# Four unread products ahead of each quad's gate and up, from quad 15 on

## Chip, cores and metric

The kernel runs on one core of one Trainium2 chip. The metric is the device time of one execution in microseconds, the median of several runs.

## What is computed

One layer on x of 16 x 256 tokens with 128 features: cross attention (16 heads of 8) to a context of 64 positions, added to x, and then a mixture of experts behind a second layer norm: a shared expert, and 64 routed experts of which each token takes 6. The routed half is what the change touches:

```python
x = x + xattn(layernorm(x), ctx_768, Wq, bq, Wk, bk, Wv, bv, Wo, bo)
x = x + moe(layernorm(x))
# moe, T = 4096 tokens, E = 64 experts, K = 6 a token, in 8 groups of which 4 stay
shared = silu(x @ sg_w.T) * (x @ su_w.T) @ sd_w.T
scores = sigmoid(x @ gate_w.T) + gate_bias
topk_w, topk_i = top_k(scores * group_mask, 6); topk_w /= topk_w.sum() + 1e-8
h = silu(einsum('th,eih->eti', x, eg_w)) * einsum('th,eih->eti', x, eu_w)
routed = einsum('eti,ehi,te->th', h, ed_w, comb)
out = shared + routed
```

## The kernel before

The program has one hand-ordered stream of instructions for each engine, tied by semaphores. It has three parts.

*Attention and routing, 16 batches.* For each batch of 256 tokens the attention is computed, the six experts of each token are picked, and GpSimd (POOL) scatters each token's row to its place in the array `pages` in HBM (L403). A page has 128 rows, in two halves of 64 rows, and each half belongs to one expert. In all there are 224 pages, taken four at a time: 56 quads (`NQ`).

*The shared expert* for all batches, in banks `bank_r` and `bank_w` of PSUM. The last two batches are finished inside quad 0; their sums (`sh_added`) are the last use of these two banks.

*The quads.* All weights of the experts lie in SBUF. For quad q:
- SP loads the pages (L344) once the buffer of quad q - 4 is free (`packed` from DVE, `pxt_done` from PE), and stores the results of quad q - 6 behind it (L332).
- PE transposes the four pages (`page_x`, L1091) into PSUM, ACT copies them to `pxt` (L455).
- DVE packs the experts' numbers (L986, L989). DVE and ACT copy the weights of these experts to `gu_now` and `d_now`, half each (DVE L1003, L1010; ACT L455).
- PE multiplies: gate and up (`gate_up`, 8 products, shown as 16 instructions writing `bank_s`), ACT takes the silu (`s_act`, L616), DVE multiplies with the up half (`h_t`, L1038), PE computes the down product (`down`, shown as 8 instructions to `bank_o` or `bank_q`), ACT copies the result to `y_s`.

PE's order in the loop is gate_up(q), page_x(q+1), down(q-1). ACT's order is silu(q), page copy(q+1), result copy(q-1), weights of quad q+2. DVE's is pack(q+2), h_t(q), weights of quad q+2, and then, in every second quad from `FIRST_SUM` = 15 on, `combine(n)` (L1022): the six results of each token of tile n, weighted, are added to `xb`.

POOL's part after the scatters is `gather(n)` for 32 tiles of 128 tokens: six indirect DMAs (L436) that fetch the six result rows of each token from `results` in HBM. A tile's gathers wait until the quads they need are stored, and, as there are four buffers, until the sum of tile n - 4 is made. 21 sums lie in the loop of the quads (quads 15, 17, ... 55), 11 behind it.

`mm(dst, w, v)` (L1095) is the helper by which most products are recorded, so the groups on its line are told apart by the tiles they write.

Of the kernel before, what the change touches and what calls it, by code (L numbers as in the profile page):

```python
# [19 lines left out]
BF16 = mybir.dt.bfloat16  # L20
# [6 lines left out]
P = 128  # L27
B = 16
# [30 lines left out]
FIRST_SUM = (E // HALVES + FILL) // QUAD + 4  # L59
# [18 lines left out]
def build(nc, x, ctx_cols, wq, bq, wk, bk, wv, bv, wo, bo, gate_cols, gate_bias, expert_gu, expert_d, shared_gu, shared_d, out, pages, results):  # L78
    with ExitStack() as ctx:
        def sb(name, shape, dt=F32):  # L80
            return ctx.enter_context(nc.sbuf_tensor(name, shape, dt))

        def ps(name, cols):
            return ctx.enter_context(nc.psum_tensor(name, [P, cols], F32))

        def sem(name):
            return ctx.enter_context(nc.semaphore(name))
# [6 lines left out]
        bank_w = ps("bank_w", 512)  # L94
# [14 lines left out]
        before = sb("before", [P, P])  # L109
        before_h = sb("before_h", [P, P], BF16)  # L110
        ones_h = sb("ones_h", [P, P], BF16)
        head_mask = sb("head_mask", [P, NH])
        mask_r = sb("mask_r", [P, HR])
        below = sb("below", [P, HR])
# [124 lines left out]
        sh_in, sh_silu, sh_ready, sh_done, sh_added = sem("sh_in"), sem("sh_silu"), sem("sh_ready"), sem("sh_done"), sem("sh_added")  # L239
# [410 lines left out]
        def _(dve):  # L650
            dve.memset(empty[:, :, :], 0.0).then_inc(empty_ready, 1)
            dve.wait_ge(made, MADE)
            dve.memset(fill[:, :], 0.0)
            dve.memset(ones_h[:, :], 1.0)
            for g in range(QUAD):
                dve.memset(digit[:, g:g + 1], float(E ** g))
            for j in range(2):
# [429 lines left out]
        def _(pe):  # L1087
            def transposes(outs, ins, done):
                for o, i in zip(outs, ins):
                    k = i.shape[0]  # L1090
                    last = pe.transpose(o, i, ident[0:k, 0:k])  # L1091
                last.then_inc(done, 1)

            def mm(dst, w, v):
                return pe.matmul(dst, w, v, start=True, stop=True)  # L1095

            def transpose_x(n):
                pe.wait_ge(xn_ready, TPB * (n + 1))
                if n > 0:
                    pe.wait_ge(q_ready, n)  # L1100
                    pe.wait_ge(kexp_ready, HR * n)
                    pe.wait_ge(vblk_ready, 2 * n)
                transposes([bank_q[:, t * P:(t + 1) * P] for t in range(TPB)], [xn[:, t, :] for t in range(TPB)], xt_done)
# [97 lines left out]
            def filling_body(b):  # L1201

                values(b - 1)
                if on(b - 3):
                    count_choosers(b - 3)
                transpose_x(b + 2)
                if on(b - 2):
                    transpose_x2(b - 2)
                    logits(b - 2)
                transpose_back(b - 1)  # L1210
                transpose_max(b)
                transpose_o(b - 1)
                shifted_scores(b)
                out_projection(b - 1)
                project(b + 2)
                scores(b + 1)

            def body(b):
                if filling(b):
                    filling_body(b)  # L1220
                    return
                if on(b - 1):
                    values(b - 1)
                if on(b + 2):
                    transpose_x(b + 2)
                if on(b - 3):
                    count_choosers(b - 3)
                if on(b - 1):
                    transpose_back(b - 1)
                if on(b):  # L1230
                    transpose_max(b)
                if on(b - 2):
                    transpose_x2(b - 2)
                if on(b):
                    shifted_scores(b)
                if on(b - 2):
                    logits(b - 2)
                if on(b + 2):
                    project(b + 2)
                if on(b + 1):  # L1240
                    scores(b + 1)
                if on(b - 1):
                    transpose_o(b - 1)
                    out_projection(b - 1)
# [12 lines left out]
            def page_x(q):  # L1257
                j = q % SLOTS
                pe.wait_ge(page_in[j], 16 * (q // SLOTS + 1))
                transposes([xt_ps[q % 2][:, g * P:(g + 1) * P] for g in range(QUAD)], [pg[j][:, g, 0:D] for g in range(QUAD)],  # L1260
                           pxt_done)

            def gate_up(q):
                pe.wait_ge(pxt_ready, q + 1)
                pe.wait_ge(gu_lower, q + 1)
                pe.wait_ge(gu_upper, q + 1)
                for u in range(HALVES * QUAD):
                    g, h = divmod(u, HALVES)
                    last = mm(gu_ps[q % 2][:, u * U:(u + 1) * U], gu_now[q % 2][:, g, h, :], pxt[q % 2][:, u * U:(u + 1) * U])
                last.then_inc(gu_done, 1)  # L1270

            def down(q):
                pe.wait_ge(h_ready, HALVES * (q + 1))
                pe.wait_ge(d_lower, q + 1)
                pe.wait_ge(d_upper, q + 1)
                if q >= 2:
                    pe.wait_ge(y_ready, q - 1)
                for g in range(QUAD):
                    last = mm(y_ps[q % 2][:, g * D:(g + 1) * D], h_t[q % 2][:, g, :, :].rearrange("p h t -> p (h t)"), d_now[q % 3][:, g, :])
                last.then_inc(y_done, 1)  # L1280
# [8 lines left out]
            def shared_down(b):  # L1289
                pe.wait_ge(sh_ready, b + 1)  # L1290
                if 2 <= b < SHARED_LATE:
                    pe.wait_ge(sh_added, b - 1)
                out_bank = (sh_out if b < SHARED_LATE else sh_bank)[b % 2]
                for t in range(TPB):
                    end = mm(out_bank[:, t * D:(t + 1) * D], sh_h[b % 2][:, t * P:(t + 1) * P], sd_t[:, :])
                end.then_inc(sh_done, 1)
# [17 lines left out]
            pe.wait_ge(sh_added, SHARED_LATE)  # L1314
            pe.wait_ge(h_zeroed, 2)
            for q in range(NQ):
                gate_up(q)
                if q + 1 < NQ:
                    page_x(q + 1)
                if q > 0:  # L1320
                    down(q - 1)
                if q == 0:
                    for b in range(SHARED_LATE, B):
                        shared_down(b)
# [32 lines left out]
```

## Time and profile before

| | |
|---|---|
| median of 3 runs | 854.12 us (847.09, 854.12, 857.15) |
| the profiled execution | 851.24 us, span 849.3 us |
| mean granted TensorE clock | 0.685 |
| PE busy | 488.6 us (58%), 2996 products and 2996 weight loads |
| DVE busy | 452.5 us (53%) |
| POOL busy | 388.8 us (46%) |
| ACT busy | 356.1 us (42%) |
| HBM traffic | 98 GB/s over the span |

The span is the time from the first to the last instruction on the core; the device time has 1.9 us around it. PE is the matrix engine (TensorE), DVE is VectorE, ACT ScalarE, POOL GpSimd, SP the engine that only issues DMAs here. The granted clock is a share of full speed: 1.00 is 2.4 GHz and 0.50 is 1.2 GHz. A product's end is modelled in the profile, its start is recorded. In the views by time, a row merges neighbouring instructions of one kind, and square brackets give the idle time of that engine ahead of it and what is taken to have ended it ("remote" and "issue": nothing that the profile shows).

### The profile page before, as it was taken

The page shows a single profiled execution, that of the slowest core. Times are in us where ns is not written, and L with a number is a line of the kernel's source. Part 1 is how long each engine was busy: PE and PEld are TensorE (multiplying, and loading weights), DVE is VectorE, ACT ScalarE, POOL GpSimd, SP SyncE. Part 2 cuts the span into 40 slices and gives each one's busy share as a digit, 9 for nine tenths or more (in the row PEclk, how much of TensorE's full clock was granted, in tenths as well). Part 3 has the DMA queues.
Part 4 walks back from the last instruction along what each step waited for, and adds up shares of the span by engine and source line. Part 5 has one row for each costly group of instructions (what it writes and reads, how often), then busy time and mean ns, then how long its engine had stood idle before and what let it go on. Part 6 is the DMA issues. An engine that isn't in the chain of part 4 may idle for free.

```text
span 849.3 us, 11843 instructions
## 1 busy us (share of the span) xinstructions
PE 488.6 (58%) x2996; PEld 408.4 (48%) x2996; DVE 452.5 (53%) x2313; ACT 356.1 (42%) x1002; POOL 388.8 (46%) x425
## 2 busy tenths in 40 slices
PE   4776555544476655322789866547777686674000
PEld 2554333323244433212679855547777686674000
DVE  4586665555666666564366633336555455455322
ACT  4563443433334433221169843436555555553000
POOL 2016455445655455566400253453444453445774
PEclk9975655567855555555799955768676867877555
DMA  7433221222222222121225532334444444433321
GB/s 217 159 128 106 91 95 51 77 97 100 101 100 94 91 94 63 60 66 47 82 63 138 150 100 76 99 99 127 114 121 110 116 130 107 118 104 84 83 59 49
DMA packets 89747, 84.25 MB, mean 99 GB/s; under 512 B 10256, under 2 KB 76816, under 8 KB 89680
## 3 DMA queue, kind: packets, MB, share of 16 engines
q1 hardware_dynamic: 76272, 57.93, 22.9%
q0 software_dynamic: 12288, 25.29, 10.5%
q8 instruction: 24, 0.39, 0.2%
q14 instruction: 43, 0.35, 0.1%
q10 hardware_dynamic: 1120, 0.28, 0.1%
HBM read 39.21 MB, written 44.25 MB: 98 GB/s over the span
## 4 chain that ended last, share of the span: by engine, by line
issue 30%; POOL 26%; PE 21%; ACT 9%; another core or an unknown queue 7%; DVE 4%; ACTq 1%; POOLq 0%; DMA 0%; DVEq 0%
POOL pages L403 17%; PE bank_s L1095 10%; PE bank_q L1095 4%; POOL empty L436 4%; POOL p_t L436 3%; ACT d_now L455 3%; PE bank_s L1091 2%; PE bank_o L1095 2%; POOL rstd L393 2%; ACT pxt L455 2%; ACT gu_now L455 2%; ACT s_act L616 1%; PE bank_r L1095 1%; ACTq L455 1%
## 5 line engine op out<-in xcount | busy, mean ns | idle before, releaser
L1095 PE MATMUL bank_s<-pxt,gu_now 128*128 128x64 f32 x896 | 148.3, 336 | 96.0 <-ACT pxt L455 61.0
L1095 PEld LDWEIGHTS bank_s<-pxt,gu_now 128*128 128x128 f32 x896 | 143.2, 250 | 103.0 <-ACT pxt L455 66.7
L436 POOL DMA_INDIRECT p_t<-results,place_i x96 | 90.9, 947 | 155.0 <-DMA results<-y_s 78.4
L436 POOL DMA_INDIRECT empty<-results,place_i x96 | 90.7, 945 | 89.4 <-DVE xb L1022 46.5
L1038 DVE TENSOR_TENSOR h_t<-bank_s,s_act 64x256 f32<-64x256 f32 x112 | 47.8, 427 | 134.5 <-ACT s_act L616 70.1
L403 POOL DMA_INDIRECT pages<-payload,place_i x96 | 93.3, 972 | 37.7 <-issue 27.6
L403 POOL DMA_INDIRECT pages<-pg,place_i x96 | 92.8, 966 | 31.3 <-issue 27.6
L393 POOL TENSOR_TENSOR rstd<-ve,minus_half 128x4 f32<-128x4 f32 (+1 forms) x21 | 18.5, 880 | 137.9 <-DVE ve L870 136.3
L616 ACT ACTIVATE s_act<-bank_s 64x512 f32<-64x512 f32 x56 | 33.0, 590 | 84.2 <-remote 63.6
L1194 PE MATMUL bank_o<-bias_s,ident 128*128 128x256 f32 x32 | 18.0, 661 | 82.4 <-ACT o_t L455 74.3
L477 ACT ACTIVATE p_t<-bank_s 128x512 f32<-128x512 f32 x64 | 35.6, 599 | 51.2 <-issue 26.4
L455 ACT ACTIVATE gu_now<-w_gu 128x128 f32 x224 | 51.0, 297 | 3.4 <-DVE expert_i L989 1.8
L1010 DVE COPY d_now<-w_d 64x128 f32 x224 | 36.1, 221 | 29.9 <-remote 17.6
L455 ACT ACTIVATE d_now<-w_d 64x128 f32 x224 | 50.4, 294 | 1.4
L1194 PEld LDWEIGHTS bank_o<-bias_s,ident 128*128 128x128 f32 x32 | 7.4, 288 | 88.3 <-ACT o_t L455 78.6
L1091 PE MATMUL bank_s<-ident,pg 128*128 128x128 f32 x224 | 46.2, 345 | 0.0
L1022 DVE SCALAR_TENSOR_TENSOR xb<-empty,weight,xb 128x128 f32<-128x128 f32 x96 | 33.6, 350 | 23.6 <-DMA empty<-results,place_i 20.8
L1022 DVE SCALAR_TENSOR_TENSOR xb<-p_t,weight,xb 128x128 f32<-128x128 f32 x96 | 33.7, 352 | 21.4 <-DMA p_t<-results,place_i 18.5
L1095 PE MATMUL bank_q<-d_now,h_t 128*128 128x128 f32 x224 | 44.3, 365 | 0.7 <-issue 0.7
L455 ACT ACTIVATE pxt<-bank_s 128x512 f32<-128x512 f32 x56 | 33.0, 590 | 26.3 <-remote 15.1
L822 DVE SCALAR_TENSOR_TENSOR picked<-iota_e,expert_f,row 128x64 f32<-128x64 f32 x192 | 42.1, 274 | 2.8 <-issue 2.8
L1095 PEld LDWEIGHTS bank_q<-d_now,h_t 128*128 128x128 f32 x224 | 42.5, 282 | 0.8 <-issue 0.8
(161 smaller groups left out, 1033.6 us busy)
## 6 DMA issues: line engine op xcount, KB each, us to landing
pg<-pages SPq DMA_DIRECT2D x56, 258.0 KB
results<-y_s SPq DMA_DIRECT2D x56, 256.0 KB
pages<-empty SPq DMA_DIRECT2D x18, 774.0 KB
w_gu<-in_expert_gu SPq DMA_DIRECT2D x16, 256.0 KB
w_d<-in_expert_d SPq DMA_DIRECT2D x32, 128.0 KB
out_x<-xb SPq DMA_DIRECT2D x16, 128.0 KB
xb<-in_x SPq DMA_DIRECT2D x3, 512.0 KB, 8.1
pages<-payload,place_i POOLq DMA_INDIRECT x96
```

Source lines behind the costliest of these rows:

```text
L393: pool.tensor_tensor(rstd[b % 2][:, part], ve[:, part], minus_half[:, part], ALU.pow).then_inc(rstd_done, 1)
L403: pool.indirect_dma_start(out=pages[:, :], out_offset=bass.IndirectOffsetOnAxis(ap=place_i[:, TPB * n + t, k:k + 1], axis=0), in_=payload[ ...
L436: pool.indirect_dma_start(out=ys[n % YS_SLOTS][:, k, :], out_offset=None, in_=results[0:landed * QUAD * P, :], in_offset=bass.IndirectOffs ...
L455: return act.activation(dst, src, ACT.Copy)
L477: act.activation(p_t[:, c, :], chunk[c], ACT.Exp).then_inc(p_ready, 1)
L616: act.activation(s_act[:, :, :, :].rearrange("p g h t -> p (g h t)"), gu_ps[q % 2][0:INTER, :], ACT.Silu).then_inc(act_ready, 1)
L822: place_step(n, ("pick", t, k), dve.scalar_tensor_tensor(out=picked[:, k, :], in0=iota_e[:, :], scalar=expert_f[:, t, k:k + 1], in1=row[:, ...
L1010: copied = dve.tensor_copy(d_now[q % 3][0:INTER, g, :], w_d[0:INTER, bass.ds(e, 1), :].rearrange("p e h -> p (e h)"))
L1022: part = dve.scalar_tensor_tensor(out=xt, in0=ys[n % YS_SLOTS][:, k, :], scalar=weight[:, n, k:k + 1], in1=xt, op0=ALU.mult, op1=ALU.add)
L1038: dve.tensor_tensor(h_t[q % 2][h * INTER:(h + 1) * INTER, :, h, :], gu_ps[q % 2][INTER:2 * INTER, :].rearrange("p (g h t) -> p g h t", g=Q ...
L1091: last = pe.transpose(o, i, ident[0:k, 0:k])
L1095: return pe.matmul(dst, w, v, start=True, stop=True)
```

## The change

DVE fills a new tile of ones, `warm_in` (128 x 512, bfloat16), at the start. From quad 15 on PE computes, ahead of each quad's gate_up and so behind the down product of the quad before the last, four products of the ones `ones_h` (128 x 128) with `warm_in` into `bank_w`. They wait for nothing, and nothing reads them. At quad 15 PE waits once until all 16 shared sums are made, the last reads of that bank. `NQ` is 56, so 41 quads have them: 164 products.

```diff
--- before.py
+++ after.py
@@ -109,6 +109,7 @@
         before = sb("before", [P, P])
         before_h = sb("before_h", [P, P], BF16)
         ones_h = sb("ones_h", [P, P], BF16)
+        warm_in = sb("warm_in", [P, 4 * P], BF16)
         head_mask = sb("head_mask", [P, NH])
         mask_r = sb("mask_r", [P, HR])
         below = sb("below", [P, HR])
@@ -652,6 +653,7 @@
             dve.wait_ge(made, MADE)
             dve.memset(fill[:, :], 0.0)
             dve.memset(ones_h[:, :], 1.0)
+            dve.memset(warm_in[:, :], 1.0)
             for g in range(QUAD):
                 dve.memset(digit[:, g:g + 1], float(E ** g))
             for j in range(2):
@@ -1094,6 +1096,11 @@
             def mm(dst, w, v):
                 return pe.matmul(dst, w, v, start=True, stop=True)
 
+            def keep_busy(times):
+
+                for _ in range(times):
+                    mm(bank_w[:, :], ones_h[:, :], warm_in[:, :])
+
             def transpose_x(n):
                 pe.wait_ge(xn_ready, TPB * (n + 1))
                 if n > 0:
@@ -1314,6 +1321,10 @@
             pe.wait_ge(sh_added, SHARED_LATE)
             pe.wait_ge(h_zeroed, 2)
             for q in range(NQ):
+                if q == FIRST_SUM:
+                    pe.wait_ge(sh_added, B)
+                if q >= FIRST_SUM:
+                    keep_busy(4)
                 gate_up(q)
                 if q + 1 < NQ:
                     page_x(q + 1)
```

## Rows read from the trace of the kernel before
**Rows 1.** stretch, us, busy PE, PEld, DVE, ACT, POOL, granted clock, DMA, GB/s

```profile
425.00:500.00 75.00, 59.81 (x462) 56.27 (x460) 41.51 (x205) 54.77 (x179) 11.37 (x12) 0.92 0.42 110
500.00:780.00 280.00, 197.56 (x1152) 193.10 (x1152) 136.91 (x606) 142.56 (x443) 124.51 (x132) 0.72 0.41 109
780.00:849.30 69.30, 0.00 (x0) 0.00 (x0) 23.76 (x68) 0.60 (x1) 45.71 (x49) 0.51 0.27 69
```

**Rows 2.** PE in order of time: start, us, what, count [idle before]

```profile
585.84 2.67 PE L1095 MATMUL bank_s<-pxt,gu_now 128*128 128x64 f32 x16 [2.13 <-issue]
...
605.48 3.51 PE L1095 MATMUL bank_s<-pxt,gu_now 128*128 128x64 f32 x16
...
655.68 1.91 PE L1095 MATMUL bank_q<-d_now,h_t 128*128 128x128 f32 x8
657.39 2.50 PE L1095 MATMUL bank_s<-pxt,gu_now 128*128 128x64 f32 x16
...
660.17 1.06 PE L1095 MATMUL bank_o<-d_now,h_t 128*128 128x128 f32 x8
665.00 3.27 PE L1095 MATMUL bank_s<-pxt,gu_now 128*128 128x64 f32 x16 [3.78 <-ACT pxt L455]
...
668.92 1.91 PE L1095 MATMUL bank_q<-d_now,h_t 128*128 128x128 f32 x8
...
691.05 2.13 PE L1095 MATMUL bank_s<-pxt,gu_now 128*128 128x64 f32 x16 [1.48 <-ACT pxt L455]
...
693.83 1.91 PE L1095 MATMUL bank_q<-d_now,h_t 128*128 128x128 f32 x8
```

**Rows 3.** order of time on ACT, same columns, quads stage

```profile
610.22 0.59 ACT L616 ACTIVATE s_act<-bank_s 64x512 f32<-64x512 f32 x1 [2.05 <-PE bank_s L1095]
...
663.88 0.59 ACT L616 ACTIVATE s_act<-bank_s 64x512 f32<-64x512 f32 x1 [3.79 <-remote]
...
676.18 0.59 ACT L616 ACTIVATE s_act<-bank_s 64x512 f32<-64x512 f32 x1 [2.85 <-remote]
...
688.95 0.59 ACT L616 ACTIVATE s_act<-bank_s 64x512 f32<-64x512 f32 x1 [2.68 <-remote]
...
701.25 0.59 ACT L616 ACTIVATE s_act<-bank_s 64x512 f32<-64x512 f32 x1 [3.02 <-remote]
```

**Rows 4.** order of time on POOL, gathers of the quads stage

```profile
661.58 0.94 POOL L436 DMA_INDIRECT empty<-results,place_i  x1 [0.30 <-issue]
...
675.28 0.94 POOL L436 DMA_INDIRECT empty<-results,place_i  x1 [0.30 <-issue]
...
694.11 0.94 POOL L436 DMA_INDIRECT p_t<-results,place_i  x1 [5.02 <-DVE xb L1022]
...
700.36 0.94 POOL L436 DMA_INDIRECT p_t<-results,place_i  x1 [0.30 <-issue]
```

**Rows 5.** all engines in order of time: two rows of one instant

```profile
677.63 0.60 ACT L455 ACTIVATE pxt<-bank_s 128x512 f32<-128x512 f32 x1 [0.86 <-remote]
677.67 0.36 SPq L344 DMA_DIRECT2D pg<-pages  x1
```

**Rows 6.** granted clock and PE busy in slices of one us

```profile
665.00:666.00 1.00, 1.00 (x7) 0.73 0.61 127
...
587.00:588.00 1.00, 1.00 (x7) 0.50 0.75 202
```

**Rows 7.** PE before the quads: float32 products of 256 columns

```profile
425.02 1.03 PE L1095 MATMUL bank_w<-x_all,sgu_t 128*128 128x256 f32 x4
425.89 0.61 PE L1095 MATMUL bank_q<-sd_t,sh_h 128*128 128x128 f32 x4
```

**Rows 8.** instructions on bank_w by line: ns min/median/max, first and last start

```profile
L1066 DVE TENSOR_TENSOR xb<-bank_w,xb x1: 411/411/411, 439.8 to 439.8; 128x256 f32<-128x256 f32 x1
```

**Rows 9.** order of time, the last sum

```profile
842.74 2.29 DVE L1022 SCALAR_TENSOR_TENSOR xb<-empty,weight,xb 128x128 f32<-128x128 f32 x6 [5.18 <-DMA empty<-results,place_i]
```

**Rows 10.** groups of DVE by line and form, first 20 us

```profile
L658 DVE MEMSET h_t<- 128x512 f32 x2 | 1.0, 485 | 0.1
```

## The prediction

> **What bounds the kernel now.** I read the busy time by stage first [rows 1]. The attention and routing stage is untouched by the diff, so it is left aside. The quads that the change touches, 15 to 55, run from 500 to about 780 us: PE is busy for 198 of the 280 us there, at a mean granted clock of 0.72, ACT for 143, DVE for 137, POOL for 125. No engine is full, so the stage is a chain of waits. Behind it lie 69 us in which PE does nothing at all and POOL and DVE gather and add the last tiles [rows 1]. That tail begins with the sum that follows quad 55 and ends with the last sum [rows 9]; it moves with the end of the quads, one for one.
>
> Next I read the quads in order of time, one engine after another. The pattern repeats every two quads, because one sum (and so one run of six gathers) goes with two quads. Four things are to be seen.
>
> First, PE's own part. When a copied page is ready, PE runs gate and up (665.00), the transposes of the next page, and the down product of the quad before (668.92, to 670.83) [rows 2]: 5.8 us at the lower clock. Then comes the other gate and up of the pair without a pause (657.39 starts as the down of 655.68 ends), its down ends at 661.23 (660.17 plus 1.06), and PE is idle until 665.00: 3.8 us [rows 2].
>
> Second, ACT idles before its silu of the second quad of each pair: 3.79, 2.85, 2.68 and 3.02 us in four that follow each other, with a releaser that the trace doesn't name [rows 3]. The gate and up it needs ended at 659.89 (657.39 plus 2.50), and ACT started at 663.88, 4.0 us later [rows 2, 3]. SP shows the same lateness: its page load at 677.67 and ACT's page copy at 677.63 start together [rows 5], two queues that share only the wait for PE's transposes.
>
> Third, what ends these idle times is the run of gathers. The last gather of a run is issued at 675.28 and ACT goes on at 676.18 (0.90 later); 700.36 and 701.25 (0.89); 661.58 and 663.88 (2.30, by then that gather should have landed) [rows 3, 4]. That is a coincidence in time, not a mechanism that I can name.
>
> Fourth, the pace. From silu to silu it is 676.18 minus 663.88 = 12.30 us with a PE part of 5.8 us, and 701.25 minus 688.95 = 12.30 us with a PE part of 4.7 us (691.05 to 693.83 plus 1.91) [rows 2, 3]. PE was 1.1 us quicker and nothing came of it. The pair is made of about 5.2 us from ACT's start to the first gather (688.95 to 694.11, by way of silu, product, copies and the sum on DVE), 6.25 us to the last gather's issue (700.36) and 0.9 us more [rows 3, 4]. PE's clock is in none of these. So my reading is that the gathers pace the quads, and PE has slack.
>
> **The change, part by part.** *The products.* From quad 15 on, 41 quads get four products of 128 by 128 times 512 columns in bfloat16: 164. The trace shows none of this form. The nearest rows are float32 products of 256 columns: four of them take 0.87 us from start to start (425.02 to 425.89) at the higher clock [rows 7], so about 1.7 us at the lower, by the halving of the clock. Below, a bfloat16 column may cost half a float32 one, with twice the columns here: the same 0.87. If it costs as much as a float32 column, it is 1.7 and 3.5 us. I take 0.87 and 1.7, since work per product is likeliest equal. In all 41 times 0.87 = 36 us to 41 times 1.7 = 70 us of PE work.
>
> Where do they lie? They stand behind the down product and ahead of the wait for the copied page. In the first quad of a pair PE is idle there for 3.8 us, and they are hidden whole. In the second there is no pause, so gate and up, the transposes and the down behind it start 0.87 to 1.7 us later. Who waits for them is ACT (silu, page copy, result copy), DVE's copy of the next down weights and SP's page load. They have 4.0 us to spare in the pair at 657.39. The least I found is 1.2 us: the gate and up at 605.48 ends at 608.99, ACT starts at 610.22 [rows 2, 3]. There 1.7 us would be late by 0.5 us. Cost on the path: 0 to about 1 us in the whole stage. Without that cover it would be 20 times 0.87 to 1.7, which is a rival below.
>
> *What the clock gives back.* The products shorten PE's idle time from 3.8 to 2.9 us and fill what is left of the pair more densely, so the mean clock should rise from 0.72, I guess to about 0.8. It will hardly hold throughout: the clock also fell after an idle time of only 2.13 us (before 585.84, low by 587), as it did at 665 after 3.78: the slice from 665 stands at 0.73 on its way down, the one from 587 at 0.50, which is 1.2 of 2.4 GHz [rows 2, 6]. By the fourth point above, a faster PE part gives nothing: 0 us.
> The Trainium skill ("TensorE: Matmul & The Clock Gate", section "Why this matters for your kernels") speaks for the change: it asks for no long idle gaps between bursts, else the clock falls to half. The trace disagrees in part, since it fell after 2.13 us. By that rule the clock would hold with gaps of 2.9 us, and if PE were on the path the time would be that of the first rival.
>
> *The wait at quad 15* for the last shared sum: the read of that bank starts at 439.8 us [rows 8], 60 us before quad 15. 0 us. It also makes the bank free.
>
> *The memset* of 128 by 512 bfloat16 early on DVE: the float32 one of that shape takes 485 ns [rows 10], and it may be anything from nothing to that. I take 0.25 us. *No DMA* is added. The 328 more instructions (164 products with their weight loads) are 5% more than the 5,992 that PE has; I see no PE idle time that their fetch would explain, so 0.
>
> **The sum.** 851.2 us (the profiled run) + 0.25 (memset) + 0 (products, hidden) - 0 (clock, off the path) = 851.5. The median shown is 2.9 us above the profiled run, which gives 854 us.
>
> **The rivals.** *PE is on the path after all, and the clock pays (faster).* For it: PE's idle time ends with ACT's page copy each time [rows 2], and that copy needs PE's transposes; if ACT's late start has to do with PE and not with the gathers, PE, ACT, PE is the loop. Against it: the equal paces of 12.30 us. The price: the part of 5.8 us at the higher clock is about 5.8 times 1.06/1.91 (down product at the higher and lower clock) [rows 2] = 3.2 us, 2.6 us less, for 20 pairs 52 us. As the clock falls again in some pairs, I give it half: 26 us, so 828 us.
>
> *The second quad's products are not hidden (slower).* The late signals of PE to ACT and SP may mean that PE really ends later than its modelled rows say. Then there is no 4.0 us to spare, and each pair pays for the four products ahead of its second gate and up: 20 times 0.87 = 17 us, so 871 us; at the lower clock 20 times 1.7 = 34 us, 888 us. It decides once the true slack is under 0.87 us. Against it: after 663.88 ACT takes the page copy and PE starts at 665.00 at once, which a PE with work left could not [rows 2, 3].
>
> *It does nothing* is the forecast itself in its result, and would also hold if the clock did not rise at all.
>
> **How the numbers follow.** Forecast (gathers pace, products hidden) 0.54, its own range 847 to 861 by the spread of the runs shown; PE on the path 0.28 (828, down to 802 if the clock holds in all pairs); not hidden 0.18 (871, up to 888). A measurement of this kernel can tell about 1% from no change, 8.5 us. So faster 0.28, same 0.54, slower 0.18. The range from 826 to 872 leaves out about half of each rival, some 0.2.
>
> **What would show it.** In the changed profile: a PE group that writes bank_w from the ones, 164 times, at 0.87 us per four; a mean clock from 500 us on above 0.72; ACT's silu of the second quad still starting 0.9 or 2.3 us after the last gather's issue, 12.3 to 14 us apart; the tail of 69 us unchanged. I would be wrong if that pace fell below 12 us with the clock (first rival), or if ACT's idle before the silu was released by PE's gate and up (second).

## The result and the profile after

The changed kernel took 857.28 us in the median of twelve runs (852.95 to 867.08), the kernel before 850.67 us (840.70 to 860.99) in twelve beside it. The ratio is **1.0094 [1.0062, 1.0127]**: slower by 0.9%, some 8 us (the medians are 6.6 us apart). The forecast was 854 us and no change. The time lies in its range, which was 46 us wide, but the interval lies wholly above 1, and the forecast's reason for "no change", that the products are hidden, has to be looked at.

The kernels ran in two sorts of jobs, and within a job all kernels had the same sort: in the **long sort** the kernel before takes 851 to 871 us, as it did when the prediction was made, in the **short sort** 633 to 635 us. In the experiments one chip was seen in both sorts, in different jobs; the other four ran in one sort each. Times are compared within a job only, and each experiment says its sort. The ratios leave slow runs out; where that choice moves a ratio much, the ratio of the means over all runs stands beside it.

The stretches of the profile after, of which the middle one answers to [rows 1] (stretch, us, busy PE, PEld, DVE, ACT, POOL, granted clock, DMA, GB/s):

```profile
425.00:500.00 75.00, 60.22 (x471) 55.68 (x469) 41.80 (x206) 54.89 (x178) 11.39 (x12) 0.94 0.42 111
500.00:785.00 285.00, 221.41 (x1312) 191.19 (x1312) 139.01 (x610) 142.56 (x445) 125.23 (x132) 0.78 0.42 107
785.00:853.00 68.00, 0.00 (x0) 0.00 (x0) 22.70 (x65) 0.00 (x0) 45.62 (x48) 0.50 0.26 70
```

PE does more and at a higher clock (0.78 against 0.72 in [rows 1]), and it takes longer all the same. The span grew from 849.3 to 853.4 us, by 4.1. Where it grew is seen at the last quad's silu and at the last sum. The kernel before, ACT in order of time:

```profile
776.82 0.59 ACT L616 ACTIVATE s_act<-bank_s 64x512 f32<-64x512 f32 x1 [1.14 <-issue]
```

The kernel after, ACT and DVE in order of time:

```profile
780.67 0.59 ACT L617 ACTIVATE s_act<-bank_s 64x512 f32<-64x512 f32 x1 [2.52 <-PE bank_s L1097]
...
846.83 2.29 DVE L1024 SCALAR_TENSOR_TENSOR xb<-empty,weight,xb 128x128 f32<-128x128 f32 x6 [5.20 <-DMA empty<-results,place_i]
```

The last silu is 3.85 us later and the last sum 4.09 us later (842.74 in [rows 9]); quad 15 begins at 500.20. So the loss arises in quads 15 to 55, and the tail is as long as before (66.2 us from the last silu to the last sum, 65.9 before).

PE after, in order of time, around three gate and ups that follow PE's idle time (answering to [rows 2]):

```profile
600.50 1.03 PE L1097 MATMUL bank_w<-warm_in,ones_h 128*128 128x512 bf16 x4
603.82 3.68 PE L1097 MATMUL bank_s<-pxt,gu_now 128*128 128x64 f32 x16 [2.29 <-ACT pxt L456]
607.28 1.06 PE L1093 MATMUL bank_s<-ident,pg 128*128 128x128 f32 x4
608.14 1.91 PE L1097 MATMUL bank_q<-d_now,h_t 128*128 128x128 f32 x8
609.85 1.43 PE L1097 MATMUL bank_w<-warm_in,ones_h 128*128 128x512 bf16 x4
611.11 1.90 PE L1097 MATMUL bank_s<-pxt,gu_now 128*128 128x64 f32 x16
...
630.35 2.00 PE L1097 MATMUL bank_s<-pxt,gu_now 128*128 128x64 f32 x16 [1.43 <-ACT pxt L456]
...
693.39 2.00 PE L1097 MATMUL bank_s<-pxt,gu_now 128*128 128x64 f32 x16 [2.82 <-ACT pxt L456]
```

The products ahead of the even quad (600.50) lie in idle time: PE still waits 2.29 us behind them for the copied page. Those ahead of the odd quad (609.85) lie in PE's unbroken work, and gate and up follows 1.26 us after their start. That is the odd quad's delay.

ACT's silu of three odd quads, each behind the last gather of a run (answering to [rows 3]):

```profile
602.69 0.59 ACT L617 ACTIVATE s_act<-bank_s 64x512 f32<-64x512 f32 x1 [3.86 <-remote]
...
615.50 0.59 ACT L617 ACTIVATE s_act<-bank_s 64x512 f32<-64x512 f32 x1 [2.96 <-remote]
...
629.23 0.59 ACT L617 ACTIVATE s_act<-bank_s 64x512 f32<-64x512 f32 x1 [2.90 <-remote]
```

POOL's last gather of the same three runs (answering to [rows 4]):

```profile
600.45 0.95 POOL L437 DMA_INDIRECT p_t<-results,place_i  x1 [0.30 <-issue]
...
614.62 0.94 POOL L437 DMA_INDIRECT empty<-results,place_i  x1 [0.30 <-issue]
...
627.02 0.95 POOL L437 DMA_INDIRECT empty<-results,place_i  x1 [0.30 <-issue]
```

The silu still goes on either about 0.9 us after the last gather's issue (615.50 less 614.62 is 0.88) or about 2.2 (2.24 and 2.21 for the other two), as in the kernel before. I counted this for the odd quads from 15 on whose silu starts within 3 us behind a run's last gather: in the kernel before 4 of 11 came late (more than 1.9 us), mean 1.44 us; after, 6 of 10, mean 1.74. In the kernel before, a pair that goes from one such silu to a late one takes 14.2 to 14.4 us, and to an early one 12.2 to 12.8 (13.5 to the one at 1.58), so a late one costs some 1.4 us at least. Two more late ones make about 3 us, and from the silu of quad 15 to that of quad 55 these two executions are 3.7 us apart. These are small counts of one execution each; the experiments had to show whether it is so.

The picture holds for about half of the quads only. Of the other ten odd silus in the kernel before, five start 0.03 or 0.04 us after the modelled end of their gate and up, one has PE named as its releaser, and four go on inside a run, with nothing named, 0.5 to 1.0 us after the issue of its fourth, fifth or seventh gather. From odd silu to odd silu the kernel before takes between 8.9 and 20.4 us, the changed one between 7.5 and 21.3.

### The profile page after: what moved, and what is told of

Read it like the earlier page. It is cut to its first block, busy times and chain, and to the rows that moved or that the text cites. A ratio compares the mean times of both kernels' runs of the same rounds, so it can differ in the third digit from the quotient of the medians.

```text
span 853.4 us, 12172 instructions
## 1 busy us (share of the span) xinstructions
PE 515.5 (60%) x3160; PEld 407.5 (48%) x3160; DVE 454.5 (53%) x2314; ACT 355.2 (42%) x1002; POOL 389.7 (46%) x425
## 4 chain that ended last, share of the span: by engine, by line
issue 27%; POOL 24%; PE 21%; another core or an unknown queue 10%; ACT 10%; DVE 5%; ACTq 2%; POOLq 0%; DVEq 0%; DMA 0%
POOL pages L404 17%; PE bank_s L1097 10%; PE bank_q L1097 4%; ACT d_now L456 3%; POOL p_t L437 3%; POOL empty L437 2%; PE bank_s L1093 2%; ACT gu_now L456 2%; PE bank_w L1097 2%; POOL rstd L394 2%; ACT pxt L456 2%; ACT s_act L617 1%; PE bank_o L1097 1%; ACTq L456 1%
## 5 line engine op out<-in xcount | busy, mean ns | idle before, releaser
L1097 PE MATMUL bank_s<-pxt,gu_now 128*128 128x64 f32 x896 | 136.5, 317 | 74.0 <-ACT pxt L456 47.4
L1097 PEld LDWEIGHTS bank_s<-pxt,gu_now 128*128 128x128 f32 x896 | 132.1, 231 | 91.9 <-ACT pxt L456 58.1
L1097 PE MATMUL bank_w<-warm_in,ones_h 128*128 128x512 bf16 x164 | 50.0, 432 | 0.4 <-issue 0.3
L688 DVE TENSOR_REDUCE minus_max<-bank_s 128x16 f32<-128x1024 f32 x32 | 37.6, 1217 | 10.2 <-PE bank_s L1097 10.2
L1097 PE MATMUL bank_q<-d_now,h_t 128*128 128x128 f32 x224 | 41.7, 348 | 0.9 <-DVE h_t L1040 0.9
```

Source lines behind the costliest of these rows:

```text
L688: dve.tensor_reduce(minus_max[:, j, :].rearrange("p (r u s) -> p r u s", r=RG, u=2)[:, :, :, 0:2], bank_s[:, :].rearrange("p (r t u v k) - ...
```

## The experiments

My theory after the result: the odd quads' products aren't hidden, since they put off work that could start at once, while the even quads' products are hidden. The rivals: the mere presence of more PE instructions, or the wait and the memset, cost something; or the products' columns do; or the higher clock or power does. To tell them apart the products were put ahead of the odd quads alone, the even ones alone, none, made short, and made twice as many. Each edit is against the changed kernel unless said.

### The first set: the short sort

No products, but the wait and the memset kept:

```diff
-                if q >= FIRST_SUM:
-                    keep_busy(4)
```

> No products; the memset and the one wait at quad 15 stay. Every theory of the products expects the time of the kernel before, 1.000 within 0.5%. If the loss sits in the memset, the wait or in where the code lies, this one is slower too, by about 0.9%.

Odd quads alone, and even quads alone (there `q % 2 == 0`):

```diff
-                if q >= FIRST_SUM:
+                if q >= FIRST_SUM and q % 2 == 1:
```

> Four products ahead of the odd quads alone (21 quads). There they stand between a down product and a gate and up that could have started at once. Theory A (the odd quad's gate and up comes late, ACT's silu and with it the sum behind it come late): all of the loss is here, 1.006 to 1.012. Theory B (every added PE instruction costs while gathers run): half of it, about 1.005. Theory C (the gathers pace the quads and the loss is drift between runs): 1.000.

> Four products ahead of the even quads alone (20 quads), in time in which PE is idle in the kernel before. Theory A: no loss, and if the clock is worth anything a gain, 0.99 to 1.000. Theory B: about 1.005. Theory C: 1.000.

64 columns in place of 512, all quads:

```diff
-                    mm(bank_w[:, :], ones_h[:, :], warm_in[:, :])
+                    mm(bank_w[:, 0:64], ones_h[:, :], warm_in[:, 0:64])
```

> The same 164 products with 64 columns in place of 512, so the same number of instructions with an eighth of the columns. Theory A (delay by the time the products take): under a quarter of the loss, 1.000 to 1.003. Theory B (cost by the number of instructions): the whole loss, about 1.009. The clock should stay near 0.72 in the quads from 15 on.

The changed kernel itself once more:

> The changed kernel itself, beside the kernel before on the chip of this job. The first four runs fell on a chip on which the kernel before takes 634 us and not 851. If this one does too: theory A (the products stand ahead of work that someone waits for) expects 1.005 or more here as well, since odd quads have them as well; theory D (the loss exists only where PE's signals come late while gathers run, that is on chips of the 851 us sort) expects 1.000 within 0.4%. If it falls on the 851 us sort: 1.009 again.

All five ran in the short sort (before: 634 us), and none differs from the kernel before: 1.0022 [0.9983, 1.0061] without products, 1.0028 [0.9994, 1.0062] odd, 1.0017 [0.9978, 1.0055] even, 1.0011 [0.997, 1.0053] short, and 0.9997 [0.9968, 1.0026] for the change as it stands. So in this sort the change does nothing, and these runs can't tell the theories apart. They do show what the long sort is. The kernel without products in the short sort, PE in order of time:

```profile
472.83 2.00 PE L1097 MATMUL bank_s<-pxt,gu_now 128*128 128x64 f32 x16 [0.76 <-ACT pxt L456]
474.66 0.61 PE L1093 MATMUL bank_s<-ident,pg 128*128 128x128 f32 x4
475.10 1.06 PE L1097 MATMUL bank_q<-d_now,h_t 128*128 128x128 f32 x8
476.26 2.00 PE L1097 MATMUL bank_s<-pxt,gu_now 128*128 128x64 f32 x16
...
480.63 2.00 PE L1097 MATMUL bank_s<-pxt,gu_now 128*128 128x64 f32 x16 [1.03 <-ACT pxt L456]
```

ACT and POOL of the same kernel:

```profile
475.14 0.59 ACT L617 ACTIVATE s_act<-bank_s 64x512 f32<-64x512 f32 x1
...
475.00 0.94 POOL L437 DMA_INDIRECT empty<-results,place_i  x1 [0.30 <-issue]
476.24 1.06 POOL L437 DMA_INDIRECT empty<-results,place_i  x1 [0.30 <-issue]
```

The trace of the kernel before, in the long sort, holds the same pace for as long as no gather runs. ACT in order of time, and POOL's first gather:

```profile
476.99 0.59 ACT L616 ACTIVATE s_act<-bank_s 64x512 f32<-64x512 f32 x1
480.44 0.59 ACT L616 ACTIVATE s_act<-bank_s 64x512 f32<-64x512 f32 x1
...
498.88 0.59 ACT L616 ACTIVATE s_act<-bank_s 64x512 f32<-64x512 f32 x1 [6.16 <-remote]
...
481.73 0.98 POOL L436 DMA_INDIRECT p_t<-results,place_i  x1 [66.62 <-DMA results<-y_s]
```

Up to 480.44 its silus are about 3.5 us apart, and one more follows at 484.53; then, behind twelve gathers, the next comes 14.35 us later. So what is long in the long sort is the time beside the gathers.

In the short sort, ACT's silu of 475.14 starts 2.3 us after the start of its gate and up (472.83), while POOL issues gathers. In the long sort the silu of [rows 3] waits until the run of gathers is over. Here ACT doesn't wait for them, POOL has no pause between one tile's six and the next, and a pair of quads takes 7.80 us (472.83 to 480.63) in place of the 12.3 to 14.2 of [rows 3].

Next came half of the gathers, in the kernel before: three of each token's six result rows are fetched and added, the others left out.

```diff
-                for k in range(TOPK):
+                for k in range(3):
```

> The kernel before with three of the six rows gathered and added per token (the other three are left out), so a run is 3 gathers and not 6. If the gathers pace the quads, the time falls by what they cost there: on the 634 us sort of chip by about 32 tiles times 3 times 1.25 us less what lies idle, 60 to 100 us; on the 851 us sort by 3.7 us per pair of quads (75 us) and 3.7 us for each of 8 tiles in the tail (30 us), 100 us in all. If PE's chain paces them, the quads keep their pace and only the tail gives its 30 us.

It took 573.72 us (two runs, 567.61 and 579.83) against 634.85: 61 us less, and again in the short sort. The edit halves DVE's sums along with the gathers. So the two together count there too, but that says little of the long sort.

### The second set: the long sort

> Products ahead of the odd quads alone, once more, for a chip of the 851 us sort. There theory A (they make the odd quad's gate and up late, and ACT's silu goes on one gather later) expects the whole loss, 1.007 to 1.012; theory B (each PE instruction costs while gathers run) half, 1.005. On the 634 us sort: 1.000 again.

> Eight products ahead of each quad, 328 in all. On the 851 us sort: theory A and B both expect about twice the loss, 1.015 to 1.02. On the 634 us sort PE has 3.93 us for a quad and is already busy for nearly all of it with four; four more at 0.87 us make PE the bound from quad 15 on: 41 times up to 0.87 = up to 35 us, 1.03 to 1.055.

The odd quads' products alone gave 875.80 us against 870.02, **1.0097 [1.0062, 1.0132]** (over all runs 1.007 with 0.003 either way): about the whole loss of the change, with half of its products. Eight products ahead of every quad, `keep_busy(8)`, gave 1.0102 [1.0069, 1.0135]: twice the PE work, and no more loss. So the loss as a whole isn't in proportion to the work added, and it doesn't need the even quads' part. Counted as above, 10 of 12 silus came late in the odd kernel and 9 of 12 in that with eight products. No trace of the kernel before was taken in this job, and the changed kernel itself was not run in it.

> Four products ahead of the even quads alone, wanted on a job where the kernel before takes 850 to 870 us. Theory E (the loss is the odd quad's gate and up ending later in the run of six gathers, so that ACT's silu goes on 2.3 to 2.5 us after the last gather's issue where it was 0.9): nothing is delayed here, ratio 1.000 within 0.4%, and the silus that go on late stay under half. Theory B (each added PE instruction costs): 1.005. If a faster clock alone paid: under 0.995. Where the kernel before takes 634 us: 1.000.

> Eight products ahead of the even quads alone, about 1.7 us at the higher clock, inside 3.8 us of idle time. Theory E: hidden, 1.000 within 0.4%, and the clock in the quads rises above that of four. If the warm clock ends the odd gate and up earlier in the run, fewer late silus and a gain of up to 1%. Theory B: 1.01. Where the kernel before takes 634 us PE has no idle time left to hide them: 1.00 to 1.03.

The even quads' products alone gave 868.59 us against 871.09, a ratio of 0.9927 [0.9887, 0.9968], which rests on the lower six of twelve runs; over all twelve (855.93 to 875.73) it is 0.997 with 0.004 either way. So there is no sign of a loss, and a gain of up to 0.7% isn't settled. Eight products ahead of the even quads alone gave 860.26 us, **0.9900 [0.986, 0.994]**, over all runs 0.989: all six runs lie below all seventeen of the kernel before. Late silus were 7 of 13 with four products and 4 of 9 with eight.

This bears on the run with eight products ahead of every quad. If its even ones gain 1.0%, its odd ones must cost about 2%, more than four do. Eight ahead of the odd quads alone were not run, so whether the odd quads' price grows with their number stays open.

The stretch 510 to 790 in the profile of the kernel with eight products ahead of the even quads:

```profile
510.00:790.00 280.00, 208.83 (x1282) 182.52 (x1301) 137.12 (x600) 139.79 (x435) 124.28 (x132) 0.80 0.41 108
```

And of the kernel with eight products ahead of every quad:

```profile
510.00:790.00 280.00, 221.53 (x1384) 179.50 (x1404) 128.83 (x581) 134.89 (x427) 118.31 (x126) 0.85 0.40 105
```

The second has the higher clock (0.85 against 0.80) and gets less done in the same 280 us: 126 instructions on POOL against 132, 427 instructions on ACT against 435. So a higher clock as such isn't what makes the time; where the products stand matters.

> The kernel before with three of six rows gathered and added (three left out). On the 850 us sort: if the end of a gather run lets the silu go on, the pace of a pair falls from about 13.1 us by 3 times 1.25 us to 9.3, in all 75 us in the quads and 30 us in the tail: 100 us less. If PE's own chain of 5.8 us and ACT's work set the pace, the quads keep it and only the tail's 30 us go.

Half of the gathers (as above, three of six rows left out) in the long sort: 742.45 us against 871.09, **0.853 [0.8474, 0.8586]**, 129 us less, twice what it gave in the short sort. ACT of that kernel in order of time:

```profile
630.46 0.59 ACT L616 ACTIVATE s_act<-bank_s 64x512 f32<-64x512 f32 x1
...
639.28 0.59 ACT L616 ACTIVATE s_act<-bank_s 64x512 f32<-64x512 f32 x1 [1.86 <-remote]
...
647.72 0.59 ACT L616 ACTIVATE s_act<-bank_s 64x512 f32<-64x512 f32 x1
...
656.57 0.59 ACT L616 ACTIVATE s_act<-bank_s 64x512 f32<-64x512 f32 x1 [1.90 <-remote]
```

Its POOL:

```profile
637.48 0.95 POOL L436 DMA_INDIRECT p_t<-results,place_i  x1 [0.30 <-issue]
643.29 0.95 POOL L436 DMA_INDIRECT p_t<-results,place_i  x1 [4.87 <-DVE xb L1022]
```

From silu to silu it is 8.4 to 8.9 us in these rows, in place of the 12.3 to 14.2 of [rows 3]: three gathers of 1.25 us fewer are 3.75 us, and the pairs are 3.4 us shorter at least. From the silu of quad 15 to that of quad 55 it is 194.3 us, against 273.1 in the trace of the kernel before (from another job). The silu still goes on only after the run (639.28 is 1.80 after 637.48). So the gathers, with the sums that go with them, set the pace, as the prediction read it.

### The third set: can the delay be moved, or made small

If the odd quad's gate and up suffers from what stands ahead of it, it might be put ahead of the down product. In the kernel before, from quad 15 on, each odd quad's gate and up comes first and the down of the quad before the last behind it:

```diff
+                if q >= FIRST_SUM and q % 2 == 1:
+                    pe.wait_ge(h_ready, HALVES * (q - 1))
                 gate_up(q)
+                if q > FIRST_SUM and q % 2 == 1:
+                    down(q - 2)
                 if q + 1 < NQ:
                     page_x(q + 1)
-                if q > 0:
+                if 0 < q < FIRST_SUM + 1 or q > FIRST_SUM and q % 2 == 1:
```

> The kernel before with another order on PE from quad 15 on: the gate and up of an odd quad runs ahead of the down product of quad q-2, not behind it, so it ends 0.9 to 1.7 us earlier, and that down, the transposes and the down behind it come later. No products added. Theory E (the later this gate and up ends in the run of gathers, the later ACT's silu goes on) expects fewer late silus and 0.985 to 0.995 on the 850 us sort, 1.000 on the 634 us sort. If the late silu has nothing to do with that end: 1.000 or, as ACT's result copy now waits longer, 1.005.

It was slower by 9%, 1.0932 [1.0868, 1.0997] (692.12 against 634.86 us), in the short sort. PE in order of time:

```profile
485.88 2.00 PE L1095 MATMUL bank_s<-pxt,gu_now 128*128 128x64 f32 x16 [2.31 <-ACT pxt L455]
487.72 0.61 PE L1091 MATMUL bank_s<-ident,pg 128*128 128x128 f32 x4
489.37 1.97 PE L1095 MATMUL bank_s<-pxt,gu_now 128*128 128x64 f32 x16 [1.04 <-issue]
491.17 1.11 PE L1095 MATMUL bank_q<-d_now,h_t 128*128 128x128 f32 x8
492.12 0.60 PE L1091 MATMUL bank_s<-ident,pg 128*128 128x128 f32 x4
492.55 1.06 PE L1095 MATMUL bank_o<-d_now,h_t 128*128 128x128 f32 x8
495.92 2.00 PE L1095 MATMUL bank_s<-pxt,gu_now 128*128 128x64 f32 x16 [2.31 <-ACT pxt L455]
```

ACT in order of time:

```profile
488.69 0.58 ACT L455 ACTIVATE pxt<-bank_s 128x512 f32<-128x512 f32 x1
```

The pair is now 10.04 us (485.88 to 495.92) in place of 7.80. PE idles 1.04 us ahead of the odd quad: with no down product between the transposes (487.72) and gate and up (489.37), the copy of the page, which ends at 489.27, is not hidden any more. The wait that the edit adds, for h_t of the quad before the last, had been met at 486.3. Then PE idles 2.31 us for the next page. The order of before is the better one there; in the long sort this wasn't tried.

Then the odd quads with products of 64 columns, which make a delay of only a quarter of a microsecond, beside the kernel without products:

> Four products of 64 columns ahead of the odd quads: the instructions of the odd-only kernel with an eighth of the columns, about 0.25 us of delay. Theory E: 1.000 to 1.004 on the 850 us sort. Theory B (each added PE instruction costs while gathers run): 1.009, as with 512 columns.

> No products, the memset and the wait only, for the 850 us sort: 1.000 within 0.4%. If the loss of 1% came from memset, wait or code, it shows here.

> As for the odd quads' short products before: on the 850 us sort theory E (time of delay) 1.000 to 1.004, theory B (number of instructions) 1.009.

> On the 850 us sort: 1.000 within 0.4% unless memset, wait or code placement cost.

> Short products ahead of the odd quads. On the 850 us sort: theory E (time of delay) 1.000 to 1.004, theory B (number of instructions) 1.009.

> No products. On the 850 us sort: 1.000 within 0.4% unless memset, wait or code placement cost.

The first two pairs fell into the short sort and gave no difference: 1.0011 [0.9973, 1.0048] and 0.9997 [0.9967, 1.0027] with short products, 0.9978 [0.9942, 1.0014] and 1.0000 [0.9976, 1.0023] without. The third ran in the long sort: **1.0158 [1.0103, 1.0212]** with short products (862.83 against 850.87 us), **1.0013 [0.9981, 1.0045]** without any. The control settles that the wait and the memset cost nothing, within 0.4%. Over all runs the short products are at 1.013 with 0.005 either way, still a loss, where the theory of the delay expected 1.000 to 1.004. The rival of the number of instructions expected 1.009 here, but it expected 1.005 and 1.01 for the even quads alone too, which came to 0.997 and 0.99. A cost by the number of instructions ahead of the odd quads alone, whatever their length, fits both odd kernels; no run separates it from a delay that takes effect however short it is.

The kernel with short products, PE in order of time:

```profile
649.84 1.91 PE L1097 MATMUL bank_q<-d_now,h_t 128*128 128x128 f32 x8
651.54 0.42 PE L1097 MATMUL bank_w<-warm_in,ones_h 128*128 128x64 bf16 x4
651.78 2.49 PE L1097 MATMUL bank_s<-pxt,gu_now 128*128 128x64 f32 x16
654.10 0.60 PE L1093 MATMUL bank_s<-ident,pg 128*128 128x128 f32 x4
```

Its ACT and POOL:

```profile
657.41 0.59 ACT L617 ACTIVATE s_act<-bank_s 64x512 f32<-64x512 f32 x1 [3.17 <-remote]
...
655.08 0.95 POOL L437 DMA_INDIRECT p_t<-results,place_i  x1 [0.30 <-issue]
```

The delay is 0.24 us (651.54 to 651.78), gate and up ended by 654.10, before the last gather was issued, and the silu came 2.33 us after that issue. In this kernel 10 of 13 silus came late, mean 1.96 us; in the kernel without products, of the same job, 5 of 12, mean 1.51. Five more late ones at 1.4 us are 7 us. The two traces are 13.6 us apart from quad 15's silu to quad 55's, so the count covers about half of it.

## Why the prediction was right or wrong

**The price of the products: right.** Four take 0.86 to 0.87 us from start to start at the higher clock (532.04 to 532.90), and 1.70 at the lower (506.23 to 507.93). The profile after, costliest groups (count, busy us, mean ns):

```profile
L1097 PE MATMUL bank_w<-warm_in,ones_h 128*128 128x512 bf16 x164 | 50.0, 432 | 0.4 <-issue 0.3
```

Their 50 us lie between the 36 and 70 us of the prediction.

**The gathers pace the quads: right in the main**, and now shown by the half gathers (129 us less, pairs of 8.4 to 8.9 us), which leave the sums' share in it open. The even pace of 12.30 us was read from a few pairs; over the whole stage they take 8.9 to 20.4 us.

**Even quads hidden: right.** Even quads alone show no loss, with four products or eight.

**Odd quads hidden, "they have 4.0 us to spare", "0 to about 1 us in the whole stage": this step failed.** Odd quads alone cost 0.7 to 1.6% (6 to 13 us), by run and by the way of counting. The 4.0 us was the time between the modelled end of gate and up and ACT's start. It isn't slack that can be used: a delay of 0.24 us in it brought the loss too. Nor was 1.2 us the least. In the kernel before, five of the 21 odd silus start 0.03 or 0.04 us after that end. Ahead of four of these gate and ups PE stood idle for 4 us and more, time into which products can fall, but quad 55's followed without a pause:

```profile
774.89 1.90 PE L1095 MATMUL bank_s<-pxt,gu_now 128*128 128x64 f32 x16
```

It ends at 776.79, and ACT's silu starts at 776.82. And the prediction's own row at 610.22 names PE's `bank_s` as what ended the wait.

What the traces show beside the loss is a step. Where the silu follows a run, it goes on about 0.9 or 2.2 to 2.5 us after the last gather's issue, a few at 1.6 or 1.7. With products ahead of the odd quads 35 of 47 such silus came late (four traces), without them 20 of 45 (before, control, and the two kernels with even quads alone), at 1.4 us or more a pair. That the later step is how the loss comes about is argued, not shown: the counts are of one execution each and partly of different jobs, they cover half of the loss in the one pair of traces with a control, and in the job of the odd and the eight-product kernels the one with fewer late silus took 7 us longer from quad 15 to quad 55. The "second quad's products are not hidden" rival named the right place, but its price (20 times 0.87 = 17 us or more, in proportion to the delay) is not what was found: a delay of 0.24 us cost as much as one of 0.87 us or more.

How a small delay, or a few instructions, could pick the later step isn't settled. Within a kernel it doesn't go by when gate and up ends: in the kernel before one that ended 5.00 us into the run was followed by an early silu, and one that ended 3.78 into it by a late one.

**The clock gives nothing: partly wrong.** The granted clock rose to 0.78, near the 0.8 guessed. But with eight products ahead of the even quads alone the kernel gained 1.0%, and more work for PE is all that it adds. That the gain comes by the clock is argued, not shown: the clock was 0.80 there, and the profile with four such products, whose gain is doubtful, had 0.73. The gains and losses of even and odd also don't simply add up to the change's 0.9%.

That the clock would not hold throughout was right. After, granted clock in slices of one us (column before the last two):

```profile
605.00:606.00 1.00, 1.00 (x6) 1.00 (x6) 0.96 (x5) 0.98 (x5) 0.00 (x0) 0.50 0.87 248
...
630.50:631.50 1.00, 1.00 (x10) 1.00 (x11) 0.97 (x7) 0.98 (x5) 0.00 (x0) 1.00 0.87 213
...
694.00:695.00 1.00, 1.00 (x11) 1.00 (x11) 1.00 (x9) 0.97 (x6) 0.00 (x0) 1.00 0.82 240
```

It stood at 0.50 (1.2 GHz) after PE had idled 2.29 us before 603.82, and at 1.00 (2.4 GHz) after 1.43 us before 630.35 and after 2.82 us before 693.39. The Trainium skill ("TensorE: Matmul & The Clock Gate", section "Why this matters for your kernels") asks for no idle gaps between bursts beyond a bound that lies above all three. The gaps of 1.43 and 2.82 us agree, that of 2.29 us does not.

**The wait, the memset, the tail: right.** The kernel without products, wait and memset kept, is at 1.0013 [0.9981, 1.0045], and the tail is as long as before. The memset took 0.485 us on DVE, where 0.25 was put, at 3.3 us from the start. No run isolates the fetch of the added instructions; the kernel with eight products ahead of the even quads has 160 more products and was faster.

**The chances.** "PE on the path" (0.28) was given more than "not hidden" (0.18). What was missed is that the rows of [rows 3] and [rows 4] already showed two steps, 0.9 and 2.3 us, and no price was put on going from one to the other: 1.4 us in each of 20 pairs, 28 us, would have been the bound.

## What to carry to other kernels

Work that only keeps the matrix engine busy belongs where the engine would stand still anyway, ahead of a wait that ends last, and not ahead of work that could start at once: here, in the long sort, the one place gained up to 1%, the other lost 0.7 to 1.6%; in the short sort neither mattered. A few rounds read closely need a look at all the others: here half of them went another way. The distance between a producer's modelled end and its consumer's start is not slack until a delay has been put into it and cost nothing. Where a start falls on one of two steps, put the distance between the steps, times the number of rounds, into the range.

## What the runs showed of the hardware

The same program runs in two ways, and a chip can show both: 634 us, or 850 to 870. In the long one, engines other than PE often stand still for 3 to 4 us although the products they need are done by the profile, and mostly go on as POOL's run of indirect DMAs ends ("remote" in the rows of ACT). They can go on inside a run too: in the kernel before the silu at 597.89 comes 0.68 us after the fifth gather's issue, and POOL issues the sixth after it. In the short sort they go on at once beside the same gathers, and in the long sort the quads ahead of the first gather run as fast as there. The part with POOL's scatters is slower in the long sort as well: between 100 and 200 us PE gets through 350 products in the kernel before, and through 487 in the short sort, in the kernel without the added products, at the same granted clock of 0.62. What makes a job the one or the other, and what holds PE's signals back, no run here shows.

In the short sort PE had 0.76 to 1.03 us of idle time in a pair, and the change put two times 0.87 us of products into it without any loss. The changed kernel there, the stretch 370 to 570:

```profile
370.00:570.00 200.00, 177.69 (x1437) 161.42 (x1456) 155.72 (x686) 159.10 (x500) 143.27 (x151) 0.96 0.68 177
```

PE is busy for 89% of it at a clock of 0.96, against 160.06 us (80%) in the kernel without products. PE filled that far was still not what sets the time.
